# A routed-expert block on one core: who issues the first gathers, when the filler rows go out, and how the expert picks are batched

## The chip, the cores and the metric

The kernel runs on 1 core of a Trainium2 chip. The time is the device time in microseconds of one execution; the median of three runs is given. One execution was also taken by the hardware profiler, and all rows below come from it.

## What is computed

The input x is 16 images of 16 x 16 positions with 256 channels, 4096 tokens in all. Three steps are added to x one after the other:

```python
x = x + conv(group_norm(x))        # a spectral mix over channels
t = x as 16 sequences of 256 tokens
t = t + attention(ln(t))           # causal, one head of width 256
# experts, on ln(t): 8 experts, each token goes to its best 2
probs = softmax(ln(t) @ router_w); keep the top 2, weights sum to 1
t = t + sum_e combine[:, e] * (gelu(ln(t) @ w_fc[e]) @ w_proj[e])   # 256 -> 1024 -> 256
```

## The kernel before

Five engines run one program each, in order, and meet only at semaphores: TensorE (PE), VectorE (DVE), ScalarE (ACT), GpSimd (POOL) and SyncE (SP). The order of work is written out by hand. An engine that waits holds up everything behind it in its own program.

**Attention slots.** `run_attention` runs slots k = -2 to 16. In slot k an engine works on sequence k (queries, keys, values), on k-1 (softmax, probabilities times values, residual), on k-2 (statistics) and on k-3 (the normalised rows for the experts). ACT's part is `act_slot`, DVE's `dve_slot`, PE's `pe_slot`, POOL's `pool_slot`.

**Picks in batches.** The two experts of each token are picked on DVE for several sequences at once, as `BATCHES` says: (first sequence, number). For a batch that ends with sequence s, `pick(j, 0)` runs in slot s+2, `pick(j, 1)` and `count_picks` in slot s+3, and `where_in`, `gap_scale`, `find_slots` and `weigh` in slot s+4. Before, the batches are 4, 4, 3, 2 and 3 sequences. The fourth batch ends its work, and the last one has all of its work, in `tail_of(g)` behind the first expert groups. ACT gives the exponential of the gap (`pick_ratio`).

**Scatters.** With a batch's slots known, POOL sends each token's row of 265 numbers twice (once for each pick) into `slots`, a table in HBM that is sorted by expert: `scatter`, 64 indirect transfers of 128 rows. Of these 32 belong to the first two batches (`EARLY` = 8 sequences, semaphore `scattered_early`) and 32 to the others (`scattered_ending`). `pool_slot` issues at most 5 in a slot; the rest stand behind the slots and between the first groups (`scatter_some`).

**Expert groups.** Then 39 groups follow: 32 of 256 rows of one expert each, and 7 of 128. Every group takes its rows with one gather (`load_group`) into the single buffer `xg`, is transposed on PE (`x_transposes`), goes up (`up`, four chunks into four banks), through gelu on ACT, and down (`down`), and POOL adds the result to `out` by two indirect transfers (`add`). Matrices are split into an upper and a lower part for accuracy: ACT casts the upper parts (`fc_upper`, `proj_upper`), DVE and POOL subtract to get the lower ones (`fc_lower`, `proj_lower`; POOL has the second half of `w_proj`). The PE order in a group is `up(g)`, `x_transposes(g+1)`, `down(g)`.

**Groups planned early.** The first six groups (`AHEAD` = 6, numbers 0 to 5, called relieved) use rows of the first 8 sequences only. They start before the last picks are known. For groups 6 and on DVE works out a plan (`plan_ends`, `plan_rows`, `plan_experts`, `plan_weights`) in the tails of groups 2 to 4, and the seven half groups follow in the tails of 4 and 5. The semaphore `plan_ready` is 1 when the number of rows of each expert is known (`counts_out`, in the tail of group 1) and 2 when the whole plan is. 8 transfers from SP write 256 filler rows behind each expert's rows (`slots<-fill`).

**Gathers.** Before, ACT issues all gathers except that of group 1. Gather 0 stands in `act_slot` at k = 14, between `probs_out` and `values`, and waits there for `first_ready` and for all early scatters. Gather 6 (the first late one) stands in ACT's group 5 between the gelu chunks 1 and 2. It waits for all 64 scatters and the 8 fillers (`slots_there`).

**Weights.** The 2 MB of each expert are loaded by SP (`weights_in`), one after the other, the first five during attention and the first groups. The last three wait for `slots_there` too, as their place in SBUF is the rows' own.

Of the kernel before, what the change touches and what calls it, by code (L numbers as in the profile page):

```python
# [15 lines left out]
B, HT, WI, D = 16, 16, 16, 256  # L16
# [15 lines left out]

BATCHES = (0, 4), (4, 4), (8, 3), (11, 2), (13, 3)
BT = 2 * max(n for _, n in BATCHES)
# [23 lines left out]
AHEAD = 6  # L58
# [69 lines left out]
def hybrid_block(nc, x_tok_d, x_ch_d, time_in_d, conv_in_d, w_in_d, attn_in_d, w_ffn_d, c_ident_d, c_idft_d, c_fill_d,  # L128
                 c_ids_d, c_numbers_d, out_d, slots_d):
    with ExitStack() as ctx:  # L130
# [379 lines left out]
        def _(sp):  # L510
# [37 lines left out]
            weights_in(sp, 0)  # L548
            for n, b in enumerate(range(EARLY + 3, EARLY + 5)):
                store(b, stored_next)  # L550
                weights_in(sp, n + 1)
            for b in range(EARLY + 5, B - 1):
# [9 lines left out]

            sp.wait_ge(plan_ready, 2)
            for e in range(E):
# [3 lines left out]


            slots_there(sp)  # L570
            sp.wait_ge(xn2_ready, 2 * B)
            sp.wait_ge(pv_mm, B)
# [5 lines left out]
        def _(pool):  # L578
# [60 lines left out]
            def pool_slot(k):  # L639

                if on(k - 2) or on(k + 2):
                    root(k)
                if k == B + 1:
                    return
                room = 1 if k == B else 5
                while left and room and k >= sum(BATCHES[batch_of(left[0][0])]) + 3:
                    scatter(*left.pop(0))
                    room -= 1
# [38 lines left out]
            pool_slot(B + 1)  # L687
            scatter_some(2)
            conv_rows_gone(pool)
            pool.wait_ge(first_ready, 4)  # L690
            for g in range(AHEAD):
                proj_lower(g, range(1, 2))
                if g > 0:
                    add(g - 1)
                scatter_some(4)
                assert g < AHEAD - 2 or not left

# [11 lines left out]
        def _(act):  # L709
# [111 lines left out]
            def act_slot(k):  # L821
# [9 lines left out]
                if on(k + 1):  # L831
                    if later(k + 1):
                        act.wait_ge(t1_mm, k + 1)
                    normalise(k + 1, k, 2, xn, xn_ready)
                if on(k - 1):
                    probs_out(k - 1)
                if k == B:
# [6 lines left out]
                    cast(0, 0)  # L844
                if k == B - 2:
                    act.wait_ge(first_ready, 4)
                    act.wait_ge(scattered_early, SENT * EARLY)
                    act.sem_inc(act_passed, 1)
                    load_group(act, 0)
                if on(k):  # L850
                    values(k)
                if on(k + 1):
                    normed_in(k + 1)
                if on(k - 3):
                    normalise(k - 3, k, 0, rows[:, 2 * k - 6:2 * k - 4, :], xn2_ready)
# [63 lines left out]
            def load_planned(g):  # L919

                planned(act, g)
                if isinstance(g, int) and g == AHEAD:
                    slots_there(act)
                    act.wait_ge(idle_stored, 16)
                act.wait_ge(meta_read, g * 2)
                act.sem_inc(act_passed, 1)
                load_group(act, g)

            def act_group(g, par):
                if relieved(g):  # L930
                    proj_upper(g, 1)
                    if g == 1:
                        pick_ratio(len(BATCHES) - 1)
                    for c in range(FC // 2):
                        if g > 0 or c > 0:
                            gelu(g, c)
                            cast(g, c)
                        if g == 0 and c == 0:
                            normalise(B - 2, B + 1, 0, rows[:, 2 * B - 4:2 * B - 2, :], xn2_ready)
                        if g_on(g - 1) and c == 0:  # L940
                            outputs(g - 1)
                        if g + 1 == AHEAD and c == 1:
                            load_planned(g + 1)
                    x_upper(g + 1)
                    fc_upper(g + 1, 1 - par)
                    if g == 0:
# [42 lines left out]
        def _(dve):  # L989
# [125 lines left out]
            for o in range(WI):  # L1115
                og, j = o // 4, o % 4
                if j == 0:
                    dve.wait_ge(mix_mm, og + 1)
                quarter = slice(32 * j, 32 * j + 32)
                v.tensor_tensor(spec[:, :].rearrange("p (b t o) -> p b t o", b=B, o=WI)[:, :, :, o],  # L1120
                                banks[4 + og][quarter, 0:B * HT],
                                inv[quarter, og * HT:(og + 1) * HT].unsqueeze(1).broadcast_to([32, B, HT]),
                                ALU.mult).then_inc(spec_ready, 1)

            def tiles_of(b):
# [277 lines left out]
            def dve_slot(k):  # L1403
# [28 lines left out]
                if on(k - 1):  # L1432
                    sums_inverse(k - 1)
                    ride_in(k - 1)
                if k == EARLY + 4:
                    order_experts()
# [40 lines left out]
            n_slots, n_groups, ends, ones, whole = (counts[:, n] for n in range(5))  # L1477
            last = len(BATCHES) - 1

# [15 lines left out]

            def plan_ends():

# [5 lines left out]
                step(v.tensor_scalar(n_groups, n_groups, MAGIC, None, ALU.add))  # L1503
                step(v.tensor_scalar(n_groups, n_groups, MAGIC, None, ALU.subtract))
                step(v.tensor_tensor(n_groups, n_groups, done[:, :], ALU.subtract))
                step(v.tensor_tensor_scan(whole, ones, n_groups, 0.0, ALU.mult, ALU.add))
# [126 lines left out]
            def slot_meta(g):  # L1633
# [6 lines left out]
                              xg[:, 0:n, ROW_ID:ROW_ID + 1].bitcast(I32)).then_inc(meta_read, 1)  # L1640

            def tail_of(g):

                if g == 0:
                    find_slots(last - 1)
                    weigh(last - 1)
                    pick(last, 0)
                    pick(last, 1)
                    gap_scale(last)
                    count_picks(last)  # L1650
                    carry_out()
                if g == 1:
                    alone(counts_mm, 1)
                    where_in(last)
                    find_slots(last)
                    counts_out()
                    weigh(last)
                if g == 2:
                    plan_ends()
                if g == 3:  # L1660
                    plan_rows()
                    plan_experts()
                if g == 4:
                    plan_weights()
                    half_counts()
# [3 lines left out]
            def dve_group(g, par):  # L1669
                if relieved(g):  # L1670
                    if g > 0:
                        proj_lower(g)
                    for c in range(FC // 2):
                        if g == 0 and c == 2:
                            alone(stored_next, 16 * (B - 1 - STORED_FIRST))
                            alone(xn2_ready, 2 * B - 2)
                        hidden(g, c)
                        if g == 0 and c == 0:
                            shifts(B + 1)
                    planned(dve, g + 1)  # L1680
# [33 lines left out]
            run_attention(dve, dve_slot)  # L1714
            shifts(B)
            alone(x2_ready, 2 * B)
# [360 lines left out]
```

## Time and profile before

| | us |
|---|---|
| median of 3 runs | 699.98 |
| lowest, highest | 699.39, 700.01 |
| the profiled execution | 698.97 |
| its span, first to last instruction | 697.0 |
| busy: PE, DVE, ACT, POOL | 616.5, 490.3, 412.8, 396.9 |

The profiled execution is 1.0 us faster than the median, and 2.0 us of it lie outside the span. PE is busy for 88% of the span. From 325 to 600 us it is busy for all 275 us; in the stretch from 283 to 302 us it does nothing. In the timelines a row is one instruction or a merged run of them, with its start, its duration and, in brackets, how long the engine was idle before it and what ended that. The issue of a transfer is a row of its own on the issuing engine's queue (ACTq, SPq).

### The profile page before, as it was taken

To read this page: it belongs to the slowest core of one execution; us is meant where nothing else is said; L and a number is where in the kernel's file an instruction comes from. 1 tells how busy PE (TensorE), PEld (TensorE's weight loads), DVE (VectorE), ACT (ScalarE), POOL (GpSimd) and SP (SyncE) were. 2 spreads that over 40 slices of the span, in tenths; PEclk is the share of its full clock that TensorE was granted. 3 is DMA by queue.
4 is the path that set the end of the run, shared out by engine and by line. 5 is a ranking of instruction groups with operands and counts; after the bars stand their busy time and mean duration, and the time that the engine had idled before them with its cause. 6 is when DMAs were issued, how large, how long until landed. Compare 5 with 4: busy or idle time off the path is not lost. (4 is left out here: it accounts for less than half of the span.)

```text
span 697.0 us, 15211 instructions
## 1 busy us (share of the span) xinstructions
PE 616.5 (88%) x4666; PEld 585.5 (84%) x4666; DVE 490.3 (70%) x1177; ACT 412.8 (59%) x726; POOL 396.9 (57%) x292
## 2 busy tenths in 40 slices
PE   1796999999578899168999999999999999999993
PEld 1685888877468899167999999999999999998993
DVE  7663678788747778457878787878787878766661
ACT  2703677765259887244566666666665656656661
POOL 5101111657743888515766667676767676777773
PEclk9997999999889999769999999999999999999997
DMA  8900010224867333774231313131313131312111
GB/s 343 298 1 0 16 46 31 94 94 156 292 238 276 87 71 71 199 273 133 40 52 32 59 31 61 31 61 31 61 31 61 31 61 31 49 30 39 32 24 16
DMA packets 37594, 62.43 MB, mean 90 GB/s; under 512 B 3696, under 2 KB 32944, under 8 KB 36400
## 3 DMA queue, kind: packets, MB, share of 16 engines
q1 hardware_dynamic: 14816, 34.56, 14.2%
q0 software_dynamic: 13296, 18.00, 14.1%
q10 hardware_dynamic: 9440, 9.36, 5.1%
q8 instruction: 20, 0.33, 0.2%
q14 instruction: 22, 0.18, 0.1%
HBM read 37.02 MB, written 24.89 MB: 89 GB/s over the span
## 5 line engine op out<-in xcount | busy, mean ns | idle before, releaser
L682 POOL TENSOR_TENSOR pj_lo<-w_ffn,pj_hi 128x1024 fp32r<-128x1024 f32 x72 | 174.1, 2422 | 98.6 <-ACT pj_hi L749 98.0
L1603 DVE TENSOR_TENSOR fc_lo<-w_ffn,fc_hi 128x1024 fp32r<-128x1024 f32 x78 | 112.4, 1473 | 67.7 <-ACT fc_hi L749 66.6
L671 POOL DMA_INDIRECT out<-y,add_id x71 | 114.7, 1615 | 42.5 <-issue 41.4
L749 ACT ACTIVATE pj_hi<-w_ffn 128x1024 fp32r x78 | 82.4, 1060 | 82.7 <-PE psO L1986 69.0
L1986 PE MATMUL psP<-pj_hi,h_hi 128*128 128x256 f32 x312 | 93.2, 299 | 11.4 <-DVE h_lo L1603 8.1
L749 ACT ACTIVATE fc_hi<-w_ffn 128x1024 fp32r x78 | 79.2, 1054 | 23.1 <-issue 20.7
L1986 PE MATMUL psP<-pj_lo,h_hi 128*128 128x256 f32 x312 | 89.1, 286 | 0.0
L1986 PE MATMUL psP<-pj_hi,h_lo 128*128 128x256 f32 x312 | 88.9, 285 | 0.0
L623 POOL TENSOR_TENSOR roots<-ve,power 128x6 f32<-128x6 f32 (+2 forms) x20 | 23.1, 1155 | 104.6 <-DVE ve L1163 91.1
L633 POOL DMA_INDIRECT slots<-rows,slot x64 | 66.7, 1042 | 24.7 <-issue 23.9
L1986 PE MATMUL psO<-pj_hi,h_hi 128*128 128x256 f32 x256 | 73.4, 287 | 0.0
L1986 PE MATMUL psO<-pj_lo,h_hi 128*128 128x256 f32 x256 | 73.1, 286 | 0.0
L1986 PE MATMUL psO<-pj_hi,h_lo 128*128 128x256 f32 x256 | 72.7, 284 | 0.0
L1986 PEld LDWEIGHTS psP<-pj_hi,h_hi 128*128 128x128 f32 x312 | 59.9, 192 | 13.9 <-DVE h_lo L1603 5.3
L903 ACT ACTIVATE psT<-psT 128x512 f32<-128x512 f32 (+1 forms) x78 | 42.8, 549 | 33.0 <-PE psT L1967 21.0
L1967 PE MATMUL psT<-x_lo,fc_hi 128*128 128x256 f32 (+1 forms) x312 | 62.0, 280 | 0.0
L1967 PE MATMUL psT<-x_hi,fc_hi 128*128 128x256 f32 (+1 forms) x312 | 61.7, 279 | 0.1
L1967 PE MATMUL psT<-x_hi,fc_lo 128*128 128x256 f32 (+1 forms) x312 | 61.5, 277 | 0.0
L1986 PEld LDWEIGHTS psP<-pj_hi,h_lo 128*128 128x128 f32 x312 | 60.4, 194 | 0.0
L1603 DVE TENSOR_TENSOR h_lo<-psT,h_hi 128x512 fp32r<-128x512 f32 (+1 forms) x78 | 50.2, 644 | 14.3 <-ACT h_hi L749 12.0
L1986 PEld LDWEIGHTS psP<-pj_lo,h_hi 128*128 128x128 f32 x312 | 60.1, 193 | 0.0
L1986 PEld LDWEIGHTS psO<-pj_hi,h_lo 128*128 128x128 f32 x256 | 49.7, 194 | 0.0
(357 smaller groups left out, 1608.5 us busy)
## 6 DMA issues: line engine op xcount, KB each, us to landing
w_ffn<-in_w_ffn SPq DMA_DIRECT2D x8, 2048.0 KB
xg<-slots ACTq DMA_DIRECT2D x31, 265.0 KB
xc<-in_x_ch SPq DMA_DIRECT2D x4, 1024.0 KB, 8.6
out<-x SPq DMA_DIRECT2D x16, 256.0 KB
x<-in_x_tok SPq DMA_DIRECT2D x1, 3072.0 KB, 25.2
slots<-fill SPq DMA_DIRECT2D x9, 265.0 KB, 2.6
out<-y,add_id POOLq DMA_INDIRECT x71
w_in<-in_w_in SPq DMA_DIRECT2D x1, 1024.0 KB, 13.7
```

The source lines that it names most:

```text
L623: nc.gpsimd.tensor_tensor(roots[:, k + 2, first:end], ve[:, first:end], power[:, first:end], ALU.pow).then_inc(roots_ready, 1)
L633: nc.gpsimd.indirect_dma_start(slots_d, bass.IndirectOffsetOnAxis(ap=slot[:, n, t:t + 1], axis=0), rows[:, t, :], None).then_inc(scattered ...
L671: nc.gpsimd.indirect_dma_start(out_d, bass.IndirectOffsetOnAxis(ap=add_id[:, s:s + 1], axis=0), y[:, s, :], None, compute_op=ALU.add).then ...
L682: nc.gpsimd.tensor_tensor(pj_lo[:, 4 * a:4 * a + 4, :], w_ffn[:, bass.ds(e, 1), (2 + a) * DFF:(3 + a) * DFF].rearrange("p a (c d) -> p (a ...
L749: nc.scalar.activation(out, src, ACT.Copy, **kw).then_inc(done, 1)
L903: nc.scalar.activation(h, h, ACT.Gelu).then_inc(gelu_done, 1)
L1603: v.tensor_tensor(out, whole, upper.bitcast(F32), ALU.subtract).then_inc(done, 1)
L1967: ins = mm(hidden_in(g, c)[:, f % 2, :], w[:, hh, f * P:(f + 1) * P], m[:, hh, 0:parts_of(g) * P], start=(n == 0), stop=(n == 5))
L1986: ins = mm(bank[:, 0:D], w[:, s * P:(s + 1) * P], m[:, f, :], start=(f == 0 and n == 0), stop=(f == FC - 1 and n == 2))
```

## The change

1. `BATCHES` becomes four batches of four sequences: the third ends with sequence 11, the last with 15. Of the last two, the one that ended with sequence 12 is gone.
2. Gather 0 is issued by SP, behind the store of sequence 12 and ahead of the third expert's weights. ACT's slot 14 no longer has a wait or a gather.
3. The fillers wait for `plan_ready` 1 instead of 2.
4. Gather 6 is issued by SP, behind the fillers and ahead of the last three experts' weights; ACT's group 5 no longer has it.
5. The last picks: `pick(last, 0)` comes between chunks 1 and 2 of gelu of group 0, and `where_in`, `find_slots` and `weigh` of the last batch between chunks 1 and 2 of group 1. The plan moves forward by up to one group: its end is in the tail of group 3.
6. ACT in slot 16 and group 0: the rows of sequence 13 are normalised before `probs_out(15)`, and `proj_upper(0, 1)` and the rows of sequence 14 come after chunk 1 of gelu.
7. POOL: one slot takes 6 scatters instead of 5, 3 instead of 2 stand ahead of group 0's `proj_lower`, 7 instead of 4 behind it.

```diff
-BATCHES = (0, 4), (4, 4), (8, 3), (11, 2), (13, 3)
+BATCHES = (0, 4), (4, 4), (8, 4), (12, 4)
...
-            for n, b in enumerate(range(EARLY + 3, EARLY + 5)):
-                store(b, stored_next)
-                weights_in(sp, n + 1)
+            store(EARLY + 3, stored_next)
+            weights_in(sp, 1)
+            store(EARLY + 4, stored_next)
+            sp.wait_ge(first_ready, 4)
+            sp.wait_ge(scattered_early, SENT * EARLY)
+            load_group(sp, 0)
+            weights_in(sp, 2)
...
-            sp.wait_ge(plan_ready, 2)
+            sp.wait_ge(plan_ready, 1)
...
+            planned(sp, AHEAD)
             slots_there(sp)
+            sp.wait_ge(idle_stored, 16)
+            sp.wait_ge(xg_t_mm, AHEAD)
+            sp.wait_ge(meta_read, 2 * AHEAD)
+            load_group(sp, AHEAD)
...
-                room = 1 if k == B else 5
+                room = 1 if k == B else 6 if k == EARLY + 4 else 5
...
-            scatter_some(2)
+            scatter_some(3)
...
-                scatter_some(4)
-                assert g < AHEAD - 2 or not left
+                scatter_some(7 if g == 0 else 4)
+            assert not left
...
+                if k == B:
+                    normalise(k - 3, k, 0, rows[:, 2 * k - 6:2 * k - 4, :], xn2_ready)
                 if on(k - 1):
                     probs_out(k - 1)
...
-                if k == B - 2:
-                    act.wait_ge(first_ready, 4)
-                    act.wait_ge(scattered_early, SENT * EARLY)
-                    act.sem_inc(act_passed, 1)
-                    load_group(act, 0)
...
-                        if g == 0 and c == 0:
+                        if g == 0 and c == 1:
+                            proj_upper(g, 1)
                             normalise(B - 2, B + 1, 0, rows[:, 2 * B - 4:2 * B - 2, :], xn2_ready)
...
-                        if g + 1 == AHEAD and c == 1:
-                            load_planned(g + 1)
                     x_upper(g + 1)
+                    planned(act, g + 1)
                     fc_upper(g + 1, 1 - par)
...
+            def picks_in(g, c):
+                if g == 0 and c == 0:
+                    shifts(B + 1)
+                if g == 0 and c == 1:
+                    pick(last, 0)
+                    alone(stored_next, 16 * (B - 1 - STORED_FIRST))
+                    alone(xn2_ready, 2 * B - 2)
+                if g == 1 and c == 1:
+                    alone(counts_mm, 1)
+                    where_in(last)
+                    find_slots(last)
+                    weigh(last)
...
                 if g == 0:
-                    find_slots(last - 1)
-                    weigh(last - 1)
-                    pick(last, 0)
                     pick(last, 1)
                     gap_scale(last)
                     count_picks(last)
                     carry_out()
                 if g == 1:
-                    alone(counts_mm, 1)
-                    where_in(last)
-                    find_slots(last)
                     counts_out()
-                    weigh(last)
+                    plan_groups()
                 if g == 2:
                     plan_ends()
+                    plan_rows()
                 if g == 3:
-                    plan_rows()
                     plan_experts()
+                    plan_weights()
                 if g == 4:
-                    plan_weights()
                     half_counts()
```

`plan_groups` is the first half of the old `plan_ends` (6 instructions), split off.

## Rows read from the trace of the kernel before

**Rows 1.** Longest waits of TensorE, 220 to 420 us: us in total, times, longest.
```profile
PE psS L1945 <- DMA xg<-slots: 20.1, 1, 20.1
PE psP L1986 <- DVE h_lo L1603: 3.4, 1, 3.4
```

**Rows 2.** Timeline of SyncE's queue: start us, us, instruction, how many.
```profile
180.02 0.01 SPq L406 DMA_DIRECT2D w_ffn<-in_w_ffn  x1
...
189.61 0.01 SPq L406 DMA_DIRECT2D w_ffn<-in_w_ffn  x1
...
279.98 9.40 SPq L566 DMA_DIRECT2D slots<-fill  x8
293.93 17.70 SPq L406 DMA_DIRECT2D w_ffn<-in_w_ffn  x3
```

**Rows 3.** Longest wait of any engine between 182 and 204 us.
```profile
ACT v_b L749 <- issue: 9.4, 1, 9.4
```

**Rows 4.** Timeline of ScalarE; idle time before and its releaser in brackets.
```profile
180.87 0.21 ACT L782 ACTIVATE ratio<-gap 128x6 f32<-128x6 f32 x1 [0.87 <-DVE gap L1233]
...
182.44 0.47 ACT L749 ACTIVATE p_t<-psP 128x384 f32<-128x384 f32 x1
191.77 0.44 ACTq L444 DMA_DIRECT2D xg<-slots  x1
...
211.80 0.60 ACT L749 ACTIVATE h_hi<-psG 128x512 fp32r<-128x512 f32 x1
...
280.55 0.47 ACT L911 ACTIVATE y<-psP,slot_w 128x256 f32<-128x256 f32 x1 [1.29 <-DMA out<-y,add_id]
...
294.00 0.41 ACTq L444 DMA_DIRECT2D xg<-slots  x1
```

**Rows 5.** Timeline of GpSimd.
```profile
185.12 1.03 POOL L633 DMA_INDIRECT slots<-rows,slot  x1 [0.19 <-issue]
...
213.47 0.71 POOL L623 TENSOR_TENSOR roots<-ve,power 128x2 f32<-128x2 f32 x1 [4.17 <-DVE ve L1161]
...
215.72 0.97 POOL L633 DMA_INDIRECT slots<-rows,slot  x1 [0.30 <-issue]
216.70 2.41 POOL L682 TENSOR_TENSOR pj_lo<-w_ffn,pj_hi 128x1024 fp32r<-128x1024 f32 x1
225.77 0.99 POOL L633 DMA_INDIRECT slots<-rows,slot  x1 [6.66 <-issue]
...
231.54 2.39 POOL L682 TENSOR_TENSOR pj_lo<-w_ffn,pj_hi 128x1024 fp32r<-128x1024 f32 x1
...
276.26 1.98 POOL L671 DMA_INDIRECT out<-y,add_id  x1 [0.30 <-issue]
...
282.37 0.96 POOL L633 DMA_INDIRECT slots<-rows,slot  x1 [0.30 <-issue]
```

**Rows 6.** Timeline of VectorE: one step of a pick, the counts by expert, the end of the plan.
```profile
225.16 0.21 DVE L1216 TENSOR_TENSOR cand<-cand,attn_in 128x48 f32<-128x48 f32 x1
...
240.60 0.17 DVE L1492 CAST tail<-tail_f 128x8 int32<-128x8 f32 x1
...
278.46 0.18 DVE L1543 CAST table<-plan 128x26 int32<-128x26 f32 x1
```

**Rows 7.** Page, DMA issues: size, median us from issue to landing.
```profile
slots<-fill SPq DMA_DIRECT2D x9, 265.0 KB, 2.6
```

**Rows 8.** Timeline of TensorE.
```profile
175.13 1.96 PE L1825 MATMUL psG<-xn_t,qk_w 128*128 128x256 f32 x8
...
193.57 3.78 PE L1825 MATMUL psG<-xn_t,qk_w 128*128 128x256 f32 x8 [5.79 <-ACT xn_t L749]
...
203.87 0.63 PE L1945 MATMUL psI<-ident,xg 128*128 128x128 f32 x4
...
219.16 0.39 PE L1986 MATMUL psP<-pj_hi,h_hi 128*128 128x256 f32 x1 [0.22 <-POOL pj_lo L682]
...
302.31 1.11 PE L1945 MATMUL psS<-ident,xg 128*128 128x128 f32 x4 [20.08 <-DMA xg<-slots]
```

More of the change, by code:

```diff
@@ L853, in act_slot @@
                     normed_in(k + 1)
-                if on(k - 3):
+                if on(k - 3) and k < B:
                     normalise(k - 3, k, 0, rows[:, 2 * k - 6:2 * k - 4, :], xn2_ready)
@@ L919, in load_planned @@
             def load_planned(g):
-                planned(act, g)
-                if isinstance(g, int) and g == AHEAD:
+                if isinstance(g, int) and g == AHEAD + 1:
                     slots_there(act)
@@ L930, in act_group @@
                 if relieved(g):
-                    proj_upper(g, 1)
+                    if g > 0:
+                        proj_upper(g, 1)
                     if g == 1:
@@ L937, in act_group @@
                             cast(g, c)
-                        if g == 0 and c == 0:
+                        if g == 0 and c == 1:
+                            proj_upper(g, 1)
                             normalise(B - 2, B + 1, 0, rows[:, 2 * B - 4:2 * B - 2, :], xn2_ready)
@@ L1123, in _ @@
                                 ALU.mult).then_inc(spec_ready, 1)
+            last = len(BATCHES) - 1
             def tiles_of(b):
@@ L1434, in dve_slot @@
                     ride_in(k - 1)
+                if k == B:
+                    shifts(B)
                 if k == EARLY + 4:
@@ L1477, in _ @@
             n_slots, n_groups, ends, ones, whole = (counts[:, n] for n in range(5))
-            last = len(BATCHES) - 1
             def carry_out():
@@ L1494, in _, with plan_groups @@
             off, jump = offset[:, 2], half_units[:, 0]
-            def plan_ends():
+            def plan_groups():
                 dve.wait_ge(ones_ready, 1)
@@ L1504, in plan_ends @@
                 step(v.tensor_scalar(n_groups, n_groups, MAGIC, None, ALU.subtract))
+            def plan_ends():
                 step(v.tensor_tensor(n_groups, n_groups, done[:, :], ALU.subtract))
@@ L1673, in dve_group @@
                     for c in range(FC // 2):
-                        if g == 0 and c == 2:
-                            alone(stored_next, 16 * (B - 1 - STORED_FIRST))
-                            alone(xn2_ready, 2 * B - 2)
                         hidden(g, c)
-                        if g == 0 and c == 0:
-                            shifts(B + 1)
+                        picks_in(g, c)
                     planned(dve, g + 1)
@@ L1714, in _ @@
             run_attention(dve, dve_slot)
-            shifts(B)
             alone(x2_ready, 2 * B)
```

## The prediction, made before the changed kernel was timed

> **What bounds the kernel now.** I read the page first: PE is busy for 616.5 of 697.0 us, and in the table by stretches it is full from 325 us on. So a change can only win ahead of that point, and whatever brings the first late group forward brings the end forward by the same amount, as 33 groups follow on a full PE. Next the waits of PE by length: one wait of 20.1 us for a gather stands out [rows 1]. On PE's timeline it lies between the end of group 5's upward part (302.31 - 20.08 = 282.2) and 302.31, where the transposes of group 6 start [rows 8]. On SyncE's queue the eight fillers go out from 279.98 on, for 9.4 us, right behind the last step of the plan at 278.46 [rows 2, 6]; the weights and ACT's gather 6 leave together at 293.93 and 294.00, when the fillers have landed [rows 2, 4]. So the chain is plan, fillers, gather; the last scatter was issued at 282.37 + 0.96 = 283.3 [rows 5], ahead of the fillers' end, and did not decide.
>
> The second hole is in attention slot 14. ACT is done with `p_t` at 182.44 + 0.47 = 182.9, issues gather 0 at 191.77 and takes `v_b` up only then, an idle stretch of 9.4 us [rows 3, 4]. "Issue" as the releaser means that the row shows no engine: it is the sequencer's wait for the early scatters. PE waits 5.79 us for `xn_t` behind it, and then runs `query_keys` in 3.78 us, where the slot before took 1.96 [rows 8].
>
> **The attention part.** Gather 0 leaves ACT's program: the wait of 9.4 us goes. PE had work until 193.57 - 5.79 = 187.8 [rows 8], so not all of it is on the path; what is, is the 5.8 us that PE waited, and 3.78 - 1.96 = 1.8 us of slow matmuls after the wait: 7.6 us. Third batch: its `gap_scale` moves from slot 14 to 15, so ACT's wait of 0.87 us for `ratio` in slot 14 goes too [rows 4]; 8.5. On the other side slot 15 now holds `where_in` to `weigh` for eight tiles (some 11 instructions of about 0.2 us [rows 6], 2 to 3 us) in place of the second pick and count of the small batch (11 of the same size). DVE waited there for ACT, so that most is covered; I charge 0.5 for larger tiles. Result: 8.0 us. Bounds: 5.8 (PE's wait alone), and 9.4 + 1.8 = 11.2 if the whole ACT wait was on the path.
>
> What must keep up. Gather 0 now stands in SP's program behind the store of sequence 12 and ahead of `weights_in(2)` and the stores of 13 and 14. The last early scatter was issued by 185.12 + 1.03 = 186.2 and had landed by 191.77 [rows 4, 5]: 5.6 us. It goes out one or two scatters earlier now, so the gather can leave at about 190, when the weights of 180.02 have landed too (the next ones left at 189.61 [rows 2]). At 3.2 us (below) it is there at 193.5; the transposes of group 0 want it 8 us ahead of 203.87, at about 196 [rows 8]. Cover of some 2.5 us. Behind it the weights take 9.6 us (180.02 to 189.61), to 200, and the store of sequence 14 lands at about 202; ACT's cast(0, 0), at 211.80 before [rows 4], wants that at 203.8. Again about 2 us of cover.
>
> One rule of the Trainium skill speaks against this edit. The rows show a wait of 9.4 us and an issue of 0.44 us on ACT [rows 3, 4]. "DMA: Bandwidth & Descriptors", section "Issuing engines are not separate DMA queues", says that all issuers feed the same 16 engines, and that issuing from another one saves only the sequencer's time to initiate a transfer. By that alone the move is worth 0.44 us and not 8.0; by the row the wait ahead of the issue is what ACT gets rid of. Its own result is rival 2.
>
> **From the attention to gather 6.** The fillers now need the counts only: ready at 240.60 before, about 1 us earlier in its group now, so that they go out in groups 1 and 2 (2.1 MB under a full PE) and cost nothing there; if the cover failed, y-adds and a gather would be 3 us late (5.6 instead of 2.3 us to land, both below), within the 4 us of slack named below. The plan ends in the tail of group 3, some 12 us ahead of before. What ends last then is the last scatter, and POOL paces it. POOL's chain, still without the 8 us: root at 213.47 + 0.71 = 214.2; three scatters instead of two add 0.30 + 0.97 = 1.27, so `pj_lo(0)` starts at 218.0 and not 216.7 and ends at 220.4 [rows 5]. Then 7 scatters, whose slots are known, at 0.99 + 0.30 = 1.3 each: 229.5. Before, POOL waited 6.66 us there for the fourth batch and started group 1 at 231.54. So POOL is 2.0 us earlier; I take 1.8, as single scatters are longer. From there to the last scatter nothing changes (4 scatters in each of groups 1 to 4): 283.3 - 1.8 = 281.5. Bounds of this gain: 0 and 2.0.
>
> Landing: the add issued by 276.26 + 1.98 = 278.2 let ACT go on at 280.55, 2.3 us later [rows 4, 5]. So all scatters are in at 283.8. The upper bound is the 5.6 us above. The gather: issue 0.4, then a transfer of the same 265 KB in 2.6 us [rows 7], 0.2 for semaphores: 3.2. Upper bound: 302.31 - 294.00 = 8.3 us, with 2 MB of weights beside it [rows 4, 8]; now the weights stand behind it in the same program. I take the lower value, since the rows nearest to a queue with nothing ahead of it are these. Gather 6 is in at 287.0 instead of 302.3: 15.3 us. Bounds: 302.3 - (283.3 + 5.6 + 8.3) = 5.1, and 302.3 - (281.3 + 2.3 + 2.8) = 15.9.
>
> **What is hidden.** PE in group 0 waits for `pj_lo`, at 219.16 before and until 220.4 now [rows 8]; with a slow phase behind it 1 to 3 us. In group 1 `where_in` to `weigh` (2.5 us) delay the third `h_lo` by about 1.5 us of PE time. The earlier ratio (12 to 17 steps of 0.2 us leave the tail of group 0 ahead of it) gives about 1.8 back in group 1. These sum to 0 to 3 us on PE, which would end group 5's upward part at 281 to 283 and then waits until 287.0 anyway: they cost nothing as long as POOL's chain is the longer one, by 4 us. If it isn't, the rest is lost. Six scatters in slot 12 fall in POOL's idle time. The moved `proj_upper(0, 1)`, `normalise` and `planned` waits lie in ACT's idle time. Everything behind 302.3 hangs on gather 6 as before: the wait of 3.4 us for `h_lo` [rows 1], behind VectorE's plan of the half groups, and the full PE.
>
> **The sum.** 8.0 + 15.3 = 23.3 us. The profiled execution would take 698.97 - 23.3 = 675.7; the median stands 1.0 above it, so 676.7. I say 677.
>
> **Rivals.**
> 1. *Forecast, both holes shrink*: 677. Bounds of its own 672 to 681.
> 2. *Attention gives next to nothing*: by the rule above, or as the slot is then paced by DVE and its batch of eight tiles, or as gather 0 is late behind the weights. Against it: DVE and ACT idle in that slot. 699.98 - 15.3 - 0.4 = 684.3.
> 3. *Gather 6 stays late*: the scatters land in 5.6 us, or the gather takes the 8.3 us that it took. For it: both durations were measured; against it: both beside 2 MB transfers, which now come later. 677 + 3.3 to 677 + 5.1, 680 to 682; with both and the POOL gain 0, 687.
> 4. *PE becomes the bound at group 6*: slow phases and the new waits in groups 0 and 1 put more than 4 us on PE. At 4 us more than that, 681.
> 5. *The other side, slower*: SP is one program. If the early scatters land late, gather 0 holds the stores of 13 and 14 and the weights behind it; ACT's cast(0, 0) needs the store of 14, and all groups come behind. Each us that gather 0 leaves after 190 costs one us beyond the 2 of cover. To eat 23.3 + 2 it would have to leave after 215, against 191.77 as measured.
> 6. *No change*: the fillers' own traffic or another wait behind `slots_there` keeps gather 6 where it was, and slot 14's hole is refilled. No row supports it.
>
> **Chances.** Forecast 0.66, rival 2 0.12, rival 3 0.12, rival 4 0.05, rival 5 0.03, rival 6 0.02. Measured changes under 0.2% (1.4 us) can't be told from none. Faster: 0.95; within 0.2%: 0.02; slower: 0.03. The range reaches from the forecast's lower bound, 672, to just beyond rival 2, 685; what both rival 2 and rival 3 together, or rival 5, would give is left out.
>
> **What would show it.** Right: no idle stretch on ACT between `p_t` and `v_b` in slot 14; the `query_keys` rows of slots 14 and 15 about 12 us apart and not 18.4 [rows 8]; PE's wait for `xg` in front of group 6 of 4 to 6 us; fillers on SP's queue at about 231; gather 6 about 2.5 us behind POOL's last scatter; three scatters ahead of POOL's first `pj_lo`, seven behind it without a wait. Wrong: gather 6 leaving more than 4 us behind the last scatter (rival 3), PE's wait there near zero (rival 4), PE waiting for gather 0 or ACT for the store of 14 (rivals 2, 5).

## The result and the profile after

Three of the four runs of the changed kernel took 675.34, 675.78 and 676.96 us; the fourth, at 710.13, ran with its clock at 0.84 where the others had 0.97, and is left out of the ratio. The median of all four is 676.37 us and that of the three 675.78, against 699.68 for four runs of the kernel before on the same chip: ratio 0.967, interval 0.963 to 0.971. The forecast was 677. The profiled run took 675.34 us, with a span of 673.5.

First come the longest waits of TensorE between 160 and 420 us (us in total, times, longest), which answer to [rows 1]:

```profile
PE psP L2001 <- DVE h_lo L1615: 8.5, 3, 3.4
PE psP L2001 <- POOL pj_lo L691: 3.2, 1, 3.2
PE psS L1960 <- DMA xg<-slots: 2.7, 1, 2.7
PE psG L1982 <- DVE x_lo L1615: 2.2, 1, 2.2
```

The wait of 20.1 us for gather 6 is down to 2.7; in its place stand several of 2 to 3 us. SyncE's queue, for [rows 2]:

```profile
185.90 0.39 SPq L444 DMA_DIRECT2D xg<-slots  x1
187.05 0.36 SPq L406 DMA_DIRECT2D w_ffn<-in_w_ffn  x1
187.46 4.69 SPq L540 DMA_DIRECT2D out<-x  x2
...
230.43 8.37 SPq L570 DMA_DIRECT2D slots<-fill  x8
275.61 0.40 SPq L444 DMA_DIRECT2D xg<-slots  x1
276.85 18.65 SPq L406 DMA_DIRECT2D w_ffn<-in_w_ffn  x3
```

Both gathers are issued here, and the fillers leave 50 us earlier (230.43, where it was 279.98). On ScalarE in slot 14, `v_b` now starts where `p_t` ends, and no idle stretch is shown [rows 3, 4]; TensorE's `query_keys` of slots 14 and 15 are 12.6 us apart and take 1.9 us each, where they were 18.4 apart and the second took 3.78 [rows 8]:

```profile
178.45 0.49 ACT L758 ACTIVATE p_t<-psP 128x384 f32<-128x384 f32 x1
178.82 0.40 ACT L758 ACTIVATE v_b<-psV 128x272 f32<-128x272 f32 x1
```
```profile
171.45 1.89 PE L1840 MATMUL psG<-xn_t,qk_w 128*128 128x256 f32 x8
...
184.05 1.95 PE L1840 MATMUL psG<-xn_t,qk_w 128*128 128x256 f32 x8
...
209.43 0.39 PE L2001 MATMUL psP<-pj_hi,h_hi 128*128 128x256 f32 x1 [3.17 <-POOL pj_lo L691]
...
251.22 0.55 PE L2001 MATMUL psP<-pj_hi,h_hi 128*128 128x256 f32 x1 [3.21 <-DVE h_lo L1615]
...
278.56 1.11 PE L1960 MATMUL psS<-ident,xg 128*128 128x128 f32 x4 [2.66 <-DMA xg<-slots]
```

GpSimd, for [rows 5]: the last square root of the attention, the `pj_lo` of groups 0 and 4, the last scatter.

```profile
202.50 0.72 POOL L632 TENSOR_TENSOR roots<-ve,power 128x2 f32<-128x2 f32 x1 [4.24 <-DVE ve L1169]
...
207.00 2.37 POOL L691 TENSOR_TENSOR pj_lo<-w_ffn,pj_hi 128x1024 fp32r<-128x1024 f32 x1
...
259.86 3.12 POOL L691 TENSOR_TENSOR pj_lo<-w_ffn,pj_hi 128x1024 fp32r<-128x1024 f32 x1 [1.81 <-ACT pj_hi L758]
...
272.22 0.96 POOL L642 DMA_INDIRECT slots<-rows,slot  x1 [0.30 <-issue]
```

With these marks every trace of this study can be cut into the same four stretches. A is from VectorE's first attention maximum (`nmax`; 71.97 us before, 70.78 after) to the start of the last root, B from there to the end of the last scatter, C from there to the start of group 6's transposes on TensorE, D what is left of the span. "Median" is of all runs of a kernel, all other columns are of its one profiled execution.

```
kernel                                       median   run    A      B     C     D
before                                       699.68  698.97 141.5  69.9  19.0  394.7
e1  before + gather 0 on SyncE               692.44  691.27 137.8  68.8  18.5  393.4
e2  before + early fills                     692.59  693.83 141.6  69.7  12.4  395.3
e3  e2 + gather 6 on SyncE                   685.45  685.20 141.6  69.6   5.2  394.9
e4  e3 + gather 0 on SyncE                   686.03  687.43 142.9  70.0   5.2  395.8
e8  e4 + one scatter in slot 14, not five    677.48  677.66 134.1  70.4   5.3  394.6
after                                        676.37  675.34 131.7  70.7   5.4  394.9
e11 after, fills wait for the plan           677.19  676.87 134.0  70.0   5.4  394.2
e12 after, gather 0 on ScalarE               687.04  689.72 137.7  72.0   5.2  402.1
e5  after, plan_rows one group later         677.73  677.47 133.6  69.7   5.7  395.4
e6  after, three scatters in slot 16         676.41  674.16 133.2  68.0   5.2  394.4
e7  e5 and e6                                676.53  679.11 133.6  66.8   9.3  395.0
e9  after, pj_lo in quarters                 678.47  679.14 134.2  70.8   5.3  394.7
e10 e9 and e6                                677.00  674.27 133.3  67.0   5.2  395.2
```

Of the 23.5 us by which the span shrank, 1.2 lie ahead of the first mark (the seven traces of changed kernels with gather 0 on SyncE and batches of four have that mark at 70.8 to 72.5: this moves from run to run), 9.8 in A, 13.6 in C; B costs 0.8 and D 0.2. The same seven traces have A at 131.7 to 134.2, so the profiled execution has the shortest of them; their mean of 133.4 puts the attention part at 8.1 us.

### The profile page after: what moved, and what is told of

Same layout as the page of the kernel before. It is cut to its first block and busy times, and to the rows that moved or that the text cites. A ratio compares the mean times of both kernels' runs of the same rounds, so it can differ in the third digit from the quotient of the medians.

```text
span 673.5 us, 15164 instructions
## 1 busy us (share of the span) xinstructions
PE 615.7 (91%) x4662; PEld 586.9 (87%) x4662; DVE 484.9 (72%) x1148; ACT 413.3 (61%) x725; POOL 395.9 (59%) x288
## 3 DMA queue, kind: packets, MB, share of 16 engines
q0 software_dynamic: 13296, 18.00, 14.6%
## 5 line engine op out<-in xcount | busy, mean ns | idle before, releaser
L1615 DVE TENSOR_TENSOR fc_lo<-w_ffn,fc_hi 128x1024 fp32r<-128x1024 f32 x78 | 109.7, 1438 | 68.0 <-ACT fc_hi L758 65.4
L680 POOL DMA_INDIRECT out<-y,add_id x71 | 113.1, 1593 | 42.6 <-issue 40.6
```

Source lines behind the costliest of these rows:

```text
L680: nc.gpsimd.indirect_dma_start(out_d, bass.IndirectOffsetOnAxis(ap=add_id[:, s:s + 1], axis=0), y[:, s, :], None, compute_op=ALU.add).then ...
L1615: v.tensor_tensor(out, whole, upper.bitcast(F32), ALU.subtract).then_inc(done, 1)
```

## The experiments

Each was timed in three rounds against the kernel before (e7 in five), which took 698.1 to 698.6 us in these sets. The changed kernel was not timed again beside them, so that a comparison with its 676.37 us goes across sets, and differences of 1 or 2 us to it mean nothing.

**e1 to e4: the two holes alone, with the old batches and picks.**

```
# e1: SyncE's program; the ACT block with load_group(act, 0) goes
+            sp.wait_ge(first_ready, 4)
+            sp.wait_ge(scattered_early, SENT * EARLY)
+            load_group(sp, 0)
             weights_in(sp, 2)
# e2
-            sp.wait_ge(plan_ready, 2)
+            sp.wait_ge(plan_ready, 1)
# e3: e2, and gather 6 behind the fills on SyncE, not on ACT
+            load_group(sp, AHEAD)
# e4: e1 + e3
```

> The kernel before with one edit: gather 0 is issued by SP and not by ACT. Theory (ACT's program order is what costs): PE's wait of 5.8 us for xn_t and 1.8 us of slow matmuls go, 7.6 us, so about 692. Rival (only the 0.44 us of issue is saved): 699.3. Second rival (gather 0 late on SP): PE shows a wait for xg of group 0 and the gain is under 5 us.

> The kernel before with one edit: the fillers wait for the counts only. ACT still issues gather 6. Theory (the last scatter is next, and a gather beside 2 MB of weights takes 8.3 us): the gather leaves 2.4 us behind the last scatter, 285.7, and lands at 294 instead of 302.3: 8.3 us, about 691.5. Rival (the gather takes 3 us wherever it stands): 13.6 us, 686. Rival (fillers were not what it waited for): 699.7.

> As the run before it, and gather 6 is issued by SP ahead of the weights. Theory: it lands 2.4 + 3.0 us behind the last scatter, 288.7 instead of 302.3: 13.6 us, about 686, that is 5 us faster than with the fillers alone. Rival (the order on the queue does not matter): the same time as with the fillers alone.

> The kernel before with the two gathers on SP and the early fillers; the five batches, the picks behind the groups and the scatter pattern stay as they were. Theory: the two parts add, 7.6 + 13.6 = 21 us, about 678.5, and the batches, moved picks and scatters are worth the last 2 us of the change. Rival (the batches and moved picks carry a large part, as POOL and DVE pace the first groups): 682 or slower. Rival (they cost as much as they save): the changed kernel's 676.4.

Measured: e1 692.44 us (ratio 0.992, 0.990 to 0.995), e2 692.59 (0.992, 0.990 to 0.994), e3 685.45 (0.982, 0.979 to 0.985), e4 686.03 (0.980, 0.975 to 0.986). The times of the first three lie within 1.1 us of the expected ones, but in part because the kernel before was itself 1.9 us faster in this set (698.13): the gains were 5.7, 5.5 and 12.7 us, where 7.6, 8.3 and 13.6 were expected. Taking gather 6 off ScalarE is thus worth 7 us on top of the early fills: it leaves 2 us earlier (285.67, not 287.64) and reaches TensorE 2.8 us behind its issue and not 9.0, with the 2 MB of weights behind it. e4 did not come out: together the two holes gave 12.1 us, where the parts sum to 18.4 and 21 were expected; its four runs lie far apart (680.73 to 687.96), and the profiled one is at 687.43. On ScalarE's timeline in slot 15 of e4:

```profile
189.21 0.20 ACT L800 ACTIVATION_READ_ACCUMULATOR p_b<-psS,nmax 128x1 f32 x1
195.69 0.60 ACT L758 ACTIVATE g_t<-psG 128x512 f32<-128x512 f32 x1 [6.28 <-remote]
198.71 0.49 ACT L758 ACTIVATE p_t<-psP 128x384 f32<-128x384 f32 x1 [2.42 <-remote]
```
```profile
187.64 1.89 PE L1827 MATMUL psG<-xn_t,qk_w 128*128 128x256 f32 x8
...
199.25 1.25 PE L1886 MATMUL psO<-v_b,p_t 128*128 128x264 f32 x2 [7.56 <-ACT p_t L758]
```

`psG` was ready at 187.64 + 1.89 = 189.5, and ScalarE took it up 6.2 us later, with no engine named as releaser ("remote" in the row). SyncE shows a gap in the same time: gather 0 leaves at 188.45, the weights behind it only at 192.76. These wait for the weights sent at 175.57, which by the traffic were in: the DMA engines' busy share is 0.21 between 186 and 188 us. And GpSimd issues scatters without a break; the one at 183.92 is the last early one, the others are the third batch's:

```profile
183.92 1.03 POOL L642 DMA_INDIRECT slots<-rows,slot  x1 [0.20 <-issue]
185.25 0.97 POOL L642 DMA_INDIRECT slots<-rows,slot  x1 [0.31 <-issue]
186.53 0.97 POOL L642 DMA_INDIRECT slots<-rows,slot  x1 [0.30 <-issue]
187.81 0.97 POOL L642 DMA_INDIRECT slots<-rows,slot  x1 [0.30 <-issue]
189.09 0.97 POOL L642 DMA_INDIRECT slots<-rows,slot  x1 [0.30 <-issue]
```

In the changed kernel GpSimd issues none between 180.5 and 189.05: a third batch of four sequences is ready one slot later than one of three, and with six scatters in slot 12 the early ones are all out by then.

**e8: e4 with four of the five scatters moved out of slot 14.**

```
-                room = 1 if k == B else 5
+                room = 1 if k in (B, B - 2) else 5
...
-                scatter_some(4)
+                scatter_some(8 if g == 0 else 4)
```

> The kernel of e4_both_holes_old_batches (old batches, gather 0 and gather 6 on SyncE, early fills: 686.0) with one thing changed: no scatters in attention slot 14, and instead eight in place of four in group 0. Theory A (scatters of the third batch, together with gather 0 and 2 MB of weights, crowd the DMA engines in slots 14 and 15, and something that needs them, most likely program code, is late for ScalarE: its idle of 6.3 us with no engine as releaser in slot 15): that idle falls under 1.5 us, slots 14 to 15 take 12 us in place of 17.1, and the time is 680 to 681. Rival B (the gap comes from something else, the order of the picks on VectorE or the short batches): the idle stays at 6 us and the time at 686. Rival C (scatters and gap are cured but eight scatters in group 0 hold POOL's pj_lo of group 1 up): the idle is gone, a wait of PE for pj_lo of group 1 of 3 to 4 us comes in its place, 683 to 684.

Measured: 677.48 us (ratio 0.971, 0.969 to 0.974), 8.6 us less than e4, whose fastest run (680.73) is slower than the slowest of e8 (680.28), and within 1.1 us of the changed kernel. `nmax` of slots 14 and 15 starts at 187.48 and 195.95, 8.5 apart and not 17.1, and the stall is gone; its two waits on ScalarE (6.28 and 2.42 us) are about the size of the gain. So what the batches of four are worth beside the two holes, they are worth by one side effect: slot 14 has no scatters of the third batch. Why that matters is not settled, and crowding as theory A has it is not what the traces show. In e8 five scatters go out from 190.59 on, beside gather 0 (189.67) and 2 MB of weights (190.84), in the changed kernel from 189.05 on beside 185.90 and 187.05, and no engine stands still for it; in e4 the stall begins at 189.4, when no weights are under way, and the DMA engines' busy share is 0.52 and 0.58 in the two stretches of 2 us from 188 on. What ScalarE was waiting for is open. I took it for late program code. In e4 the profile page's two queues called "instruction" (q8, q14) have no packet between 184 and 202 us, which does not speak for that; but nothing says that they are all such queues.

**e11 and e12: one part of the change undone.**

```
# e11
-            sp.wait_ge(plan_ready, 1)
+            sp.wait_ge(plan_ready, 2)
# e12: SyncE loses the gather, ACT has it back in slot B - 2
+                if k == B - 2:
+                    act.wait_ge(first_ready, 4)
+                    act.wait_ge(scattered_early, SENT * EARLY)
+                    act.sem_inc(act_passed, 1)
+                    load_group(act, 0)
```

> The changed kernel with SyncE's fills again waiting for the plan's end (plan_ready 2) and not for the counts alone. Theory A (with the plan's steps moved two groups ahead it ends at 258.9 in place of 280, so the fills would be issued from 259.5 to 268 and have landed by 270.6, ahead of the last scatter at 273.2): no change, 676.4; of the two ways to have the fills early, either is enough. Rival B (the fills' traffic meets other transfers there, or the last scatter is later by it): 678 to 680. Without the moved plan, this wait was worth 5.7 us (e2).

> The changed kernel with gather 0 issued by ScalarE in slot 14 again, as before. My prediction's term: 8.0 us for the attention part as a whole, so 684.4; by the traces 8.9, so 685.3. Theory B (e8 showed that scatters in slot 14 beside gather 0 and 2 MB of weights cost 8.6 us, and these are not there with batches of four): ScalarE's queue is less crowded and the issue is short; the 9.4 us stall was mostly this crowding, and the time is 678 to 680. Rival C: ScalarE waits for the whole issue as before, 9.4 us, and since its wait for first_ready comes later with the longer batch, 686 or more.

Measured: e11 677.19 us (ratio 0.972, 0.967 to 0.976): no difference from the changed kernel that can be told from noise. The fills left at 262.53 for 8.7 us, and the gather at 277.82 behind the last scatter at 275.42. With the plan moved ahead, the wait for counts alone gives nothing; without it, it gave 5.5 us (e2).

e12 took 687.04 us (ratio 0.983, 0.977 to 0.989), in two clusters: 683.74 and 684.36, and 689.72 and 691.12. The lower one is the 684.4 of the prediction's own term. The profile is of the upper one. Its A is 137.7, 4.3 over the mean of the seven, with the old hole on ScalarE:

```profile
187.96 0.40 ACT L755 ACTIVATE v_b<-psV 128x272 f32<-128x272 f32 x1 [7.69 <-issue]
```

Its D is 7.2 us longer than that of the changed kernel, behind 657 us, where the last groups run: a wait of 2.04 us for `fc_lo` at 664.17, and a granted clock of 0.71 from 660 to 670 and 0.61 from 670 to 680, while TensorE is busy for 8.0 and 8.4 of the 10 us; the changed kernel has 1.00 in its last such stretches, from 636 to 666. Whether this belongs to the edit or to two of its four runs, one profile can't say.

**e5, e6, e7: two waits of 3 us taken away.** TensorE's wait of 3.17 us in group 0 is for a `pj_lo` that stands behind three scatters; the one of 3.21 us in group 3 is for an `h_lo` behind the plan.

```
# e5: tail_of(g) on VectorE; plan_rows() from g == 2 to g == 3
# e6
-                room = 1 if k == B else 6 if k == EARLY + 4 else 5
+                room = 4 if k == B else 6 if k == EARLY + 4 else 5
...
-            scatter_some(3)
# e7: both
```

> The changed kernel with one step put back: plan_rows runs in DVE's tail of group 3, as before, and not in that of group 2. Theory A (the POOL term of my sum failed because plan_rows' operation on 128x208 met POOL's pj_lo of group 3 and took 2.93 us there in place of 0.38, which made h_lo of group 3 late by 3.2 us for PE and, one group on, pj_hi late by 1.8 us for POOL): PE's wait of 3.2 us for h_lo near 251 us is gone, POOL's 1.81 us before pj_lo of group 4 too, the last scatter ends near 271 us in place of 273.2, and the time is 674.4. Rival B (the operation meets POOL's pj_lo just as well one group later, or the longer tail of group 3 delays the same h_lo): the same waits stand one group on and the time stays at 676 to 677. Rival C: the plan's end comes later, the fills with it, and gather 6 too: 678 or more.

> The changed kernel with three scatters moved: they are issued in POOL's slot 16, in its idle 4.2 us ahead of the last square root, and not between that root and pj_lo of group 0. Theory A (three scatters of 1.2 us each stand in the way of pj_lo of group 0, for which PE waits 3.17 us at 209.4): PE's wait falls to under 0.5 us, POOL's whole chain of scatters and pj_lo up to gather 6 runs 3 us earlier, and the time is 672.6. Rival B (the square root itself is delayed, since the three don't fit into the idle time): 675.5. Rival C (DVE is the next that is late for group 0, or the scatters' traffic delays the attention's last slots): 676 to 677.

> The changed kernel with both: plan_rows in the tail of group 3, and the three scatters in slot 16. If the two gains are independent (each takes away a PE wait of its own of 3.2 us, in groups 0 and 3): 670.5 to 671. Rival: what is won in group 0 is given back at the late h_lo or at the wait for gather 6, where PE waited 2.7 us: then the time is that of the better of the two, 672.5 to 674.

Measured: e5 677.73 us (ratio 0.971, 0.969 to 0.973), e6 676.41 (0.971, 0.967 to 0.975), e7 676.53 (0.969, 0.967 to 0.970). None beats the changed kernel. e5 moved the wait on: TensorE waits 4.22 us for `h_lo` in group 4, where a step of the plan on 26 elements took 3.04 us. VectorE and GpSimd side by side:

```profile
260.20 0.18 DVE L1553 CAST table<-plan 128x26 int32<-128x26 f32 x1
260.42 3.04 DVE L1554 TENSOR_SCALAR plan<-plan 128x26 f32<-128x26 f32 x1
263.50 0.18 DVE L1555 CAST table<-plan 128x26 int32<-128x26 f32 x1
```
```profile
261.05 2.36 POOL L691 TENSOR_TENSOR pj_lo<-w_ffn,pj_hi 128x1024 fp32r<-128x1024 f32 x1
```

It ends at 263.46, GpSimd's subtraction at 263.41. The changed kernel has the same in group 3:

```profile
243.78 0.38 DVE L1531 TENSOR_TENSOR past<-numbers,counts 128x208 f32<-128x208 f32 x1 [0.17 <-issue]
244.19 2.93 DVE L1532 TENSOR_TENSOR past_sum<-past,half_units 128x208 f32<-128x208 f32 x1
247.15 0.37 DVE L1533 TENSOR_REDUCE plan<-past_sum 128x26 f32<-128x208 f32 x1
```
```profile
244.46 2.42 POOL L691 TENSOR_TENSOR pj_lo<-w_ffn,pj_hi 128x1024 fp32r<-128x1024 f32 x1
```

e6 shortened B by 2.7 us in its profile, the best of all by span (672.3), but not its median: its runs go from 674.16 to 681.60. The wait of 3.17 us in group 0 did not fall to under 0.5 as expected; TensorE waits there 2.26 us for `h_lo`, as now a step of the picks meets GpSimd's subtraction:

```profile
206.13 0.21 DVE L1221 TENSOR_REDUCE best<-logits 128x8 f32<-128x64 f32 x1
206.38 2.05 DVE L1222 TENSOR_TENSOR cand<-logits,best 128x64 f32<-128x64 f32 x1
```
```profile
205.94 2.40 POOL L691 TENSOR_TENSOR pj_lo<-w_ffn,pj_hi 128x1024 fp32r<-128x1024 f32 x1 [0.53 <-issue]
```

In e7 the same step takes 2.21 us. e7 brought the last scatter's end 3.8 us forward in B and gave that back in C (9.3 us): gather 6 left at 275.53, but TensorE, with a wait of 4.76 us for `h_lo` in group 4, reached its transposes at 282.32 only.

**e9, e10: the long subtraction in four pieces.**

```
# e9, groups 0 to 5
-                    nc.gpsimd.tensor_tensor(pj_lo[:, 4 * a:4 * a + 4, :], ...)
+                        for q in range(4):
+                            part = nc.gpsimd.tensor_tensor(
+                                pj_lo[:, 4 * a + q:4 * a + q + 1, :], ...)
+                        part.then_inc(pj_lo_ready[a], 1)
# e10: e9 + e6
```

> The changed kernel with POOL's pj_lo of groups 0 to 5 written as four subtractions of 128x256 each in place of one of 128x1024. Theory A (an operation of DVE that starts just ahead of POOL's long subtraction is held until that is over: past_sum, 2.93 us, ended at 247.12 where POOL's pj_lo ended at 246.88; in e5 a plan operation of 26 elements took 3.04 us and ended at 263.46, POOL's at 263.41): no small operation of DVE takes over 1 us in the groups' tails, PE's wait for h_lo in group 3 falls from 3.2 us to under 1.5 and POOL's wait of 1.8 us for pj_hi of group 4 goes; the last scatter ends 1.8 us earlier, and the time is 674.5. Rival B (the two engines only happen to end together): the operation of DVE keeps its 2.9 us and the time stays at 676.4. Rival C (four subtractions take POOL much longer than 2.4 us, so its chain to gather 6 is later): 678 or more.

> As e9, and three scatters moved into POOL's slot 16 as in e6. Theory A: both waits of about 3 us that PE has in groups 0 and 3 are smaller, gather 6 can start with the last scatter some 3 us earlier: 673. Rival B: gather 6 and what follows it (weights of the first late expert) hold the end, and both stay at 676: the early waits were slack.

Measured: e9 678.47 us (ratio 0.971, 0.968 to 0.974), e10 677.00 (0.970, 0.967 to 0.973). VectorE and GpSimd of e10 in group 0, with the steps that e6 has there; VectorE in group 3, GpSimd in groups 3 to 5, and TensorE in front of group 6:

```profile
206.43 0.21 DVE L1229 TENSOR_REDUCE best<-logits 128x8 f32<-128x64 f32 x1
206.68 0.23 DVE L1230 TENSOR_TENSOR cand<-logits,best 128x64 f32<-128x64 f32 x1
206.94 0.65 DVE L1231 TENSOR_TENSOR cand<-cand,attn_in 128x64 f32<-128x64 f32 x1
```
```profile
206.07 2.83 POOL L693 TENSOR_TENSOR pj_lo<-w_ffn,pj_hi 128x256 fp32r<-128x256 f32 x4 [0.36 <-ACT pj_hi L765]
```

```profile
242.49 0.37 DVE L1539 TENSOR_TENSOR past_sum<-past,half_units 128x208 f32<-128x208 f32 x1
```
```profile
245.90 3.00 POOL L693 TENSOR_TENSOR pj_lo<-w_ffn,pj_hi 128x256 fp32r<-128x256 f32 x4
...
259.01 2.81 POOL L693 TENSOR_TENSOR pj_lo<-w_ffn,pj_hi 128x256 fp32r<-128x256 f32 x4
...
272.01 2.77 POOL L693 TENSOR_TENSOR pj_lo<-w_ffn,pj_hi 128x256 fp32r<-128x256 f32 x4
```
```profile
PE psS L1967 <- DMA xg<-slots: 6.4, 1, 6.4
```

No small step of VectorE in groups 0 to 5 takes over 1 us any more, and the wait for `h_lo` in group 3 is gone. That tests the hold in group 0. e10 is e6 with the subtraction in four pieces: in both, VectorE's pick steps start some 0.2 to 0.4 us behind its start. Where e6 has one step of 2.05 us, e10 has none over 0.66, about the length of one piece, and TensorE's wait there is 1.41 us and not 2.26. In group 3 nothing is tested: GpSimd's `pj_lo` starts at 245.90, when VectorE's steps of the plan had ended at 244.2, and in groups 4 and 5 they don't meet either. So the hold of theory A is borne out, but the 674.5 and 673 us that it promised were not reached; e9's time is that of rival C. TensorE waits for gather 6 instead, 6.4 us and not 2.7. The scatters' chain on GpSimd, 13.0 to 13.1 us a group here with hardly a gap, ends B, and the four pieces take it 0.4 to 0.6 us longer in each group. What TensorE gains ahead of group 6 is slack as long as GpSimd has 26 scatters (23 in e10), five `pj_lo` and the adds of four groups between the last root and the last scatter.

## Why the prediction was right, point by point

**The sum.** 23.3 us were forecast; measured are 699.68 - 676.37 = 23.3, or 23.9 by the median of the three runs. By the profiled executions the attention part gave 1.8 us more than its term, the part up to gather 6 gave 2.5 less, and 1.2 lie ahead of the first mark, which moves by that much from run to run. So the agreement to 0.6 us is partly luck. The two holes are those that the prediction names; what closed the first one is only in part what it says.

**The attention part**, 8.0 us: 8.1 by the mean of seven traces, 9.8 by the profiled one. The wait and the slow matmuls behind it are gone; the wait for `ratio` is not, it stands in slot 15 now (0.77 us). But the working put 7.6 us on the gather's move and next to nothing on the batches. With the old batches the move took 3.7 us out of A and 5.7 out of the median (e1), and beside the other moves it took nothing (e4 against e3). With the new ones it took 4.3 out of A, and 10.7 out of the median with e12's upper runs in it, 7.7 by the mean of its lower two (684.05). The step "third batch" was priced by its instructions (0.9 gained on ScalarE, 0.5 lost on VectorE); its worth lay in when GpSimd's scatters run. 8.6 us hang on that by e4 and e8, of the 9.7 by which e4 and the changed kernel differ, and no term of the sum has it. Gather 0 could leave at about 190 by the forecast and left at 185.90: the last early scatter was out at 180.4, where it was 186.2.

**Rival 2** (the rule that an issuer saves only its time to start the transfer: 0.44 us) fell: the row had 9.4 us of waiting ahead of the issue, and e12, with the gather back on ScalarE, has 7.7 us of it again. "DMA: Bandwidth & Descriptors" of the Trainium skill speaks of the transfer, and of that the rule may well hold; the wait is in the program that issues it.

**Gather 6**, 15.3 us: B and C shrank by 12.8. The term that failed is GpSimd's chain, "I take 1.8": B grew by 0.8. The seven scatters behind `pj_lo(0)` ran as said, from 209.54 on without a wait. Counted from the root, the chain was 2.6 us earlier than before at `pj_lo` of group 3 (244.46, 42.0 us behind it, where it was 44.5). Then it lost 3.4: 2.4 up to `pj_lo` of group 4, which started 1.81 us late, and 1.0 behind that start, where `pj_lo` took 3.12 us for 2.4. "From there to the last scatter nothing changes" left out `plan_rows` in its new place: it was held by `pj_lo` of group 3 and made `h_lo` and then `pj_hi` late. This is read from the traces, and it is at most a part: in e6, where `plan_rows` met no `pj_lo`, the two `pj_lo` are still 14.6 us apart (15.4 here, 13.0 before). B of e9, where they didn't meet either, is no shorter (70.8), since the pieces take longer. And B is 68.7 to 70.0 in e1 to e4, which have the old chain: the gain that is missing is sure, the loss of 0.8 is not.

**Landing and gather.** 2.3 + 3.2 = 5.5 us were forecast, against bounds of 5.6 and 8.3; from the last scatter's end at 273.18 to 278.56 it was 5.4, and 5.2 to 5.4 in eight other traces where gather 6 stood on SyncE and TensorE was waiting. Rival 3 is out.

**What is hidden.** The cover held, by less than said: TensorE waited 2.7 us for gather 6, where 4 to 6 were forecast, since group 3's wait of 3.2 us and the matmuls at half clock behind it (0.50 between 252 and 254) had not been counted. `pj_lo(0)` was awaited until 209.4, which is the forecast 220.4 less the 11.0 by which the root is earlier. In e7 the cover was gone, and rival 4 is what one sees there.

**SyncE in order** (rival 5). Gather 0 left at 185.90 and its transposes ran at 191.71 without a wait; ScalarE's cast(0, 0) lost 0.27 us to the store in front of it. The fillers left at 230.43 (231 forecast).

## What to carry to other kernels

Price a change to the batching by when its transfers run, too, and not by its instructions alone: here the DMA-issuing engine's pattern, moved by one slot, was worth 8.6 us, more than the first hole by itself (5.7), and it only showed when the parts were built one by one and did not add up. When two edits feed one wait (plan and fills), one of them can be free. And before taking away a wait of the busiest engine, ask which chain ends at the next meeting point; e5, e6, e7, e9 and e10 each removed or moved such a wait, and none was faster than the changed kernel.

## What the runs showed of the hardware

A small step of VectorE (7 to 208 elements a partition, 0.2 to 0.4 us otherwise) that meets GpSimd's subtraction of 128x1024 can take 2.0 to 3.3 us. Steps held so start between 0.7 us ahead of the subtraction and 0.5 us behind its start, and they end with it: at 247.12 beside 246.88 and 275.67 beside 275.61 in the changed kernel, 262.96 beside 262.91 in e7, 250.71 beside 250.67 in e11, 289.52 beside 289.50 in e8. They are steps with two inputs, copies, casts and steps with a scalar. A reduction is not held: in e7 one runs from 207.61 for 0.21 us inside a subtraction that started at 207.58, and the two-input step behind it takes 2.21. Where steps and subtraction don't overlap, no step is long from 150 us to group 6 and on to 320. Cut into four, the subtraction holds a step for no more than 0.8 us (e9, e10).

The other way round, GpSimd's copy of two elements, 0.18 us, takes 1.2 in e6, e7 and the kernel before. There it ends with a subtraction of 128x1024 on VectorE (286.83 beside 286.79 before), which itself takes 3.3 us beside GpSimd's, where 1.2 are usual.

"SBUF — State Buffer", section "SBUF: two separate sides", of the Trainium skill says that the two engines share a port pair, which the instruction that starts first locks for its whole length. The trace agrees on the duration, 2.93 us beside a subtraction of 2.42. It does not show who started first: the step of VectorE has the earlier recorded start, by 0.27 us, and still ends last. Moving small steps is thus worth nothing for sure: e5 moved them out of one `pj_lo` into the next.

In e1 and e4, which have the old batches, engines stand idle in slots 14 and 15 with no engine as releaser, while scatters go out: 6.28 and 2.42 us on ScalarE in e4, 2.38 and 3.51 on VectorE in e1, where ScalarE's 5.90 follow from the second. With four scatters gone from slot 14 (e8) that went too, though scatters, gather and weights still run together in slot 15. The cause stays open.
